# A graph-network kernel on one core: small tables on ScalarE's queue, waits at first use, index transfers ahead of their tiles

## The chip, the core and the metric

The kernel runs on one core of a Trainium2 chip as one program. Its time is the device time of that core in microseconds: 4792.28 us, the median of 3 runs (4786.27 to 4793.47).

The names used here: PE is TensorE, DVE is VectorE, ACT is ScalarE, POOL is GpSimd, SP is SyncE, which only issues transfers. Each has its own instruction stream and its own queue of transfers (its "queue" below); the transfers of all queues are carried out by the core's 16 DMA engines. Between streams there are only semaphores: `.then_inc(sem, n)` raises one when an instruction is done, `wait_ge(sem, v)` holds the stream until it has reached v. All instructions behind a wait in the same stream wait too.

## The reference, cut to what matters

50,000 nodes and 25,000 edges (source, destination; sorted by destination), 128 features, all in fp32. Four layers, each of them added to x, each on h = relu(layernorm(x)):

```python
def gine(h):                        # layer 0
    agg = segment_sum(relu(h[src] + edge_attr), dst)
    y = relu((h + agg) @ W1.T + b1) @ W2.T + b2
    return batchnorm_over_nodes(y) * gamma + beta
def gatv2_conv(h):                  # twice in layer 1, edges plus a self loop per node, 4 heads
    e = einsum(leaky_relu((h @ Wl)[s] + (h @ Wr)[d]), att)
    alpha = softmax of e over the edges of each destination
    return segment_sum(alpha * (h @ Wl)[s], d).mean(heads) + bias
h1 = relu(layer_norm(gatv2_conv(h), g1, be1) + h)       # layer 1
x = x + layer_norm(gatv2_conv(h1), g2, be2) + h1
def gat(h):                         # layer 2, 4 heads of 64, no self loops
    out = relu(softmax-weighted segment_sum of (h @ W_n)[src])
    return relu(out @ mlp_W1 + mlp_b1) @ mlp_W2 + mlp_b2
x = x + 0.5 * segment_sum(h[src], dst) / max(degree, 1)   # layer 3
```

## The kernel before, in words

Nodes are padded to 98 tiles of 512 rows (256 KB each), edges to 49 tiles of 512. The program is a row of phases, each with SBUF, PSUM and semaphores of its own. A phase is one `nc.Block()`, which ends in a barrier on all engines; then `Phase.__exit__` (L53) clears the semaphores on POOL behind a second one (L58). So no instruction of a phase runs before the last one of the phase ahead is done on every engine. POOL's first instruction in a phase is the memset of the identity (`make_identity`, L122), which marks a phase's start in the profile.

In order, with their starts in the profiled execution: gine_edges 0; gine_mlp 563.6; gine_finish 877.5; conv_nodes for the layer-1 convolution 0 at 1159.2 and for the other, called final, at 1447.8; for convolution 0 conv_logits 1722.9, edge_softmax 2251.0, conv_aggregate 2290.7; for convolution 1 the same three at 2604.8, 3133.8 and 3173.5; gat_logits 3545.2; edge_softmax 3875.0; gat_aggregate 3919.2; mean_edges 4282.9.

Inside a phase each engine's stream is written as steps with lags: `sweep(N, [(lag, step), ...])` (L244) runs, for t = 0, 1, ..., step(t - lag) of each pair in the order of the list, where that tile exists. A negative lag runs a step ahead of its tile. SP issues a phase's loads several tiles ahead (rings of 7 node tiles, `tile_in[r]`; of 3 edge tiles in conv_aggregate and gat_aggregate) and its stores.

What a phase needs once, its tables, is loaded at its head. `broadcast_rows` (L98) is one transfer that reads a row of 128 features again for each of 128 partitions, 64 KB in 512-byte pieces. The tables of each phase, all on SP's queue and, but for gine_mlp (after tile 0), ahead of the tile loads:

- gine_mlp (L449): two weights, four columns of 128 (`weights_in`); DVE, PE and ACT wait for all six before anything else.
- gine_finish (L612): the row of the next layer's beta, broadcast four times (`beta_in`), which POOL adds to each tile. POOL's stream: identity, wait for beta, `iota` of row numbers, then for each tile one addition (L641) and one scatter of row numbers into the table POS by an indirect DMA (`scatter_last`, L115).
- conv_nodes (L1410): Wl (256 KB), gamma broadcast, then for convolution 0 beta broadcast four times, the bias row four times; for the final one the bias rows, mlp_row broadcast, the MLP's w2 and b1. DVE sums Wl and the bias into the mean weights `wmean` (L1503 to L1514), PE's first `turn` (transpose) waits for these, `project` (L1489) follows. In the final phase PE also makes a row from relu(b1) and w2 (L1473) ahead of its first tile, and DVE adds it to mlp_row (L1522). In the other POOL looks up POS by a gather (L111) behind each tile's addition.
- conv_logits (L786): Wl, Wr, the eight pieces of the masks KEEP and KEEPN (`Masks.load`, L720), `att`. DVE: wait for the weights, Wl + Wr, centring of Wl by head and its mean (L945 to L958), then two mask scans (L733), then the tiles; PE's first tile waits for the masks' turns (L743).
- conv_aggregate (L1167): gamma, four rows, the bias as a column (`weights_in`, 96 in all). PE, POOL and DVE wait for them at once; PE averages the bias (L1243), DVE centres it (L1325), then `weigh` (alpha by source features) and `project` (L1250) begin. In convolution 0 POOL also looks up POS twice per edge tile.
- gat_logits (L1616): W_n, a_src, a_dst, then the masks. gat_aggregate (L1777): w1, w2, b1; PE and ACT wait for these at once.

## Time and profile before

| | us |
|---|---|
| median of 3 runs | 4792.28 (4786.27 to 4793.47) |
| profiled execution | 4799.01 |
| its span | 4797.0 |
| PE busy in it | 3393.7 (71%) |
| DVE busy | 3285.1 (68%) |
| POOL busy | 2889.3 (60%) |
| ACT busy | 2668.4 (56%) |
| DMA | 1019.82 MB, mean 213 GB/s |

The rows come from one profiled execution. A row of a timeline has the start in us from the span's start, the duration, the engine ("SPq" is the issue of a transfer by SP, not the transfer), the line of the kernel, the operation and its operands (out<-in), how many instructions the row joins, and in brackets how long the engine had been idle before and whose end released it; "PEq" and "POOLq" are the engine's own sequencer at a barrier or a drain. A row of windows has, for a stretch, the busy time of each engine, the granted TensorE clock (1.00 is full), the DMA engines' busy share and their rate.

### The profile page before, as it was taken

The page shows a single profiled execution, that of the slowest core. Times are in us where ns is not written, and L with a number is a line of the kernel's source. Part 1 is how long each engine was busy: PE and PEld are TensorE (multiplying, and loading weights), DVE is VectorE, ACT ScalarE, POOL GpSimd, SP SyncE. Part 2 cuts the span into 40 slices and gives each one's busy share as a digit, 9 for nine tenths or more (in the row PEclk, how much of TensorE's full clock was granted, in tenths as well). Part 3 has the DMA queues.
Part 4 walks back from the last instruction along what each step waited for, and adds up shares of the span by engine and source line. Part 5 has one row for each costly group of instructions (what it writes and reads, how often), then busy time and mean ns, then how long its engine had stood idle before and what let it go on. Part 6 is the DMA issues. An engine that isn't in the chain of part 4 may idle for free. (4 is left out here: it accounts for less than half of the span.)

```text
span 4797.0 us, 66181 instructions
## 1 busy us (share of the span) xinstructions
PE 3393.7 (71%) x14380; PEld 1894.6 (39%) x14380; DVE 3285.1 (68%) x10437; ACT 2668.4 (56%) x7608; POOL 2889.3 (60%) x2835
## 2 busy tenths in 40 slices
PE   1544188544998979997797999948855649974332
PEld 1534133222665633432564344325532215543331
DVE  1322199775996768887786888869978868874332
ACT  1422299796776757775575777726657735530000
POOL 4777687687984457773687555315567600027776
PEclk9656599655999989998898999979978869985555
DMA  8433288796668966664896444459979956753331
GB/s 290 124 97 92 102 282 278 290 406 252 201 190 269 307 194 209 212 212 143 273 323 217 154 158 157 135 195 338 337 239 342 336 164 216 229 185 105 98 99 53
DMA packets 685509, 1019.82 MB, mean 213 GB/s; under 512 B 109779, under 2 KB 293748, under 8 KB 683248
## 3 DMA queue, kind: packets, MB, share of 16 engines
q1 hardware_dynamic: 617296, 877.29, 55.0%
q0 software_dynamic: 65856, 113.13, 9.0%
q10 hardware_dynamic: 2016, 25.69, 1.3%
q8 instruction: 112, 1.84, 0.2%
q14 instruction: 229, 1.88, 0.1%
HBM read 640.44 MB, written 381.14 MB: 213 GB/s over the span
## 5 line engine op out<-in xcount | busy, mean ns | idle before, releaser
L984 DVE TENSOR_TENSOR conv_logits_leaky<-conv_logits_z,conv_logits_sloped 128x512 f32<-128x512 f32 x784 | 516.9, 687 | 117.8 <-ACT conv_logits_sloped L918 102.0
L918 ACT ACTIVATE conv_logits_sloped<-conv_logits_z 128x512 f32<-128x512 f32 x784 | 459.1, 596 | 175.9 <-PE conv_logits_z L880 123.5
L1250 PE MATMUL conv_aggregate_part<-conv_aggregate_weighed,conv_wlc 128*128 128x512 f32 x784 | 360.0, 602 | 39.8 <-DVE conv_aggregate_weighed L1332 39.8
L880 PE MATMUL conv_logits_z<-conv_logits_hdT,conv_logits_wsum 128*128 128x512 f32 x784 | 368.0, 613 | 4.7 <-DVE conv_logits_leaky L984 2.7
L887 PE MATMUL conv_logits_z<-conv_diffT,conv_logits_wl 128*128 128x512 f32 x784 | 352.9, 593 | 0.0
L1570 ACT ACTIVATE conv_nodes_squares<-conv_nodes_o_ps 128x128 f32<-128x128 f32 x784 | 206.5, 278 | 165.7 <-PE conv_nodes_o_ps L1492 165.7
L1332 DVE TENSOR_TENSOR conv_aggregate_weighed<-conv_aggregate_alpha,conv_diffT 128x512 f32<-128x512 f32 x392 | 259.8, 722 | 9.5 <-DMA conv_aggregate_alpha<-ALPHA 9.5
L117 POOL DMA_INDIRECT AGG<-gine_edges_rows,idx x196 | 194.0, 990 | 103.1 <-issue 101.9
L1492 PEld LDWEIGHTS conv_nodes_o_ps<-conv_nodes_wmean,conv_nodes_hT 128*128 128x128 f32 x1568 | 191.3, 192 | 160.3 <-DVE conv_nodes_hT L1528 81.4
L1959 PE MATMUL mean_edges_turned<-mean_edges_ident,mean_edges_hs 128*128 128x128 f32 x196 | 54.6, 434 | 277.7 <-DMA mean_edges_hs<-H,idx 277.7
L111 POOL DMA_INDIRECT gat_logits_hs<-H,idx x196 | 214.4, 1094 | 59.8 <-issue 56.8
L2001 DVE SCALAR_TENSOR_TENSOR mean_edges_rows<-mean_edges_back,mean_edges_half,mean_edges_base 128x128 f32<-128x128 f32 x196 | 55.3, 344 | 276.1 <-DMA out<-mean_edges_rows,idx 273.8
L880 PEld LDWEIGHTS conv_logits_z<-conv_logits_hdT,conv_logits_wsum 128*128 128x128 f32 x784 | 142.9, 192 | 230.1 <-issue 216.6
L1492 PE MATMUL conv_nodes_o_ps<-conv_nodes_wmean,conv_nodes_hT 128*128 128x128 f32 x1568 | 228.9, 289 | 4.3
L117 POOL DMA_INDIRECT out<-mean_edges_rows,idx x196 | 194.7, 993 | 59.7 <-issue 59.0
L111 POOL DMA_INDIRECT gine_edges_hs<-x,idx x196 | 188.6, 962 | 65.3 <-issue 59.4
L1542 DVE SCALAR_TENSOR_TENSOR conv_nodes_scaled<-conv_nodes_o_ps,conv_nodes_rstd,conv_nodes_gamma 128x128 f32<-128x128 f32 x784 | 220.9, 345 | 7.0
L111 POOL DMA_INDIRECT conv_logits_hdx<-HX,idx x196 | 188.3, 961 | 59.9 <-issue 59.9
L111 POOL DMA_INDIRECT conv_logits_hs<-HX,idx x196 | 188.0, 959 | 59.7 <-issue 59.7
L111 POOL DMA_INDIRECT mean_edges_hs<-H,idx x196 | 187.9, 959 | 59.8 <-issue 59.8
L1489 PE MATMUL conv_nodes_o_ps<-conv_nodes_bias,conv_nodes_ones 1*128 1x512 f32 x392 | 221.8, 645 | 0.0
L661 PE MATMUL gine_finish_rows<-gine_finish_ident,gine_finish_bT 128*128 128x128 f32 x392 | 109.1, 434 | 156.9 <-ACT gine_finish_bT L695 155.5
(294 smaller groups left out, 10205.0 us busy)
## 6 DMA issues: line engine op xcount, KB each, us to landing
conv_aggregate_alpha<-ALPHA SPq DMA_DIRECT2D x392, 256.0 KB, 5.3
HX<-gine_finish_hx SPq DMA_DIRECT2D x98, 512.0 KB, 11.7
AGG<-gine_edges_zero ACTq DMA_DIRECT2D x14, 1792.0 KB, 34.2
gine_mlp_x<-x SPq DMA_DIRECT2D x98, 256.0 KB
gine_mlp_agg<-AGG SPq DMA_DIRECT2D x98, 256.0 KB
YT<-gine_mlp_yT SPq DMA_DIRECT2D x98, 256.0 KB, 4.2
gine_finish_x<-x SPq DMA_DIRECT2D x98, 256.0 KB, 7.1
gine_finish_yT<-YT SPq DMA_DIRECT2D x98, 256.0 KB, 11.5
```

Of the source, the lines that this page charges most:

```text
L111: return pool.indirect_dma_start(out=out, out_offset=None, in_=table, in_offset=bass.IndirectOffsetOnAxis(ap=index, axis=0))
L117: return pool.indirect_dma_start(out=table, out_offset=bass.IndirectOffsetOnAxis(ap=index, axis=0), in_=rows, in_offset=None, bounds_check ...
L880: pe.matmul(z[h][:, :], wsum[:, h * D:(h + 1) * D], hdT[j % 3][:, :], start=True, stop=True).then_inc(z_done[0], 1)
L887: pe.matmul(z[h][:, :], wl[:, h * D:(h + 1) * D], g.diffT[:, cols(j)], start=False, stop=True, skip_group_check=True).then_inc(z_done[1], 1)
L918: act.activation(sloped[(H * (2 * j + c) + h) % S][:, :], z[h][:, :], ACT.Copy, scale=SLOPE).then_inc(sloped_made[c], 1)
L984: dve.tensor_tensor(leaky[H * c + h][:, :], z[h][:, :], sloped[(H * (2 * j + c) + h) % S][:, :], ALU.max).then_inc(leaky_made[c], 1)
L1250: last = pe.matmul(part[n % 2][:, :], g.wlc[:, h * D:(h + 1) * D], weighed[n % 2][:, h, :], start=(h == 0), stop=(h == H - 1))
L1332: dve.tensor_tensor(weighed[n % 2][:, h, :], alpha[n % 3][:, h, :], g.diffT[:, n * TILE:(n + 1) * TILE], ALU.mult).then_inc(weighed_made, 1)
L1489: pe.matmul(flat(o), ones[:, :], bias[:, :], start=True, stop=False, skip_group_check=True)
L1492: last = pe.matmul(o[:, a, :], hT[k % 2][:, a * P:(a + 1) * P], wmean[:, :], start=False, stop=True, skip_group_check=True)
L1542: last = dve.scalar_tensor_tensor(out=scaled[r][:, a, :], in0=o_ps[n % 4][:, a, :], scalar=rstd[r][:, a:a + 1], in1=gamma[:, :], op0=ALU.m ...
L1570: last = act.activation(squares[r][:, a, :], o_ps[n % 4][:, a, :], ACT.Square, accum_out=power[r][:, a:a + 1])
```

## The change

Three kinds of edit. **Queue:** the tables listed above are issued by ACT at the head of its stream, in place of SP; in gat_logits and conv_logits that is the masks, the weights staying on SP. **Waits:** each engine waits for them in the step that first reads them. In conv_nodes the tables are split: Wl and the bias rows count on `core_in` and come first, the rest on `weights_in`; PE's row of the final phase moves into a bank of its own and behind the first tiles. In conv_logits the centring of Wl moves behind diff(0). **Look-ahead:** POOL's scatters in gine_finish run 8 tiles ahead of the additions, its gathers in conv_nodes 7 ahead, in conv_aggregate 4 ahead.

```diff
# gine_mlp
-                    if k == 0 and isinstance(i, int) and i == 0:
-                        for dst, src in ((w1, g.w1T), (w2, g.w2T), (b1, g.b1), (b2, g.b2), (gamma, g.gamma), (beta, g.beta)):
-                            sp.dma_start(dst[:, :], src).then_inc(weights_in, 16)
...
                 def copy_y(k, i):
                     r, n = k % RING, i * NB + k
+                    if k == 0 and isinstance(i, int) and i == 0:
+                        dve.wait_ge(weights_in, 6 * 16)
...
                 def first(k, i):
                     n = i * NB + k
+                    if k == 0 and isinstance(i, int) and i == 0:
+                        pe.wait_ge(weights_in, 6 * 16)
...
+                for dst, src in ((w1, g.w1T), (w2, g.w2T), (b1, g.b1), (b2, g.b2), (gamma, g.gamma), (beta, g.beta)):
+                    act.dma_start(dst[:, :], src).then_inc(weights_in, 16)
                 act.wait_ge(eps_set, 1)
-                act.wait_ge(weights_in, 6 * 16)
...
# gine_finish
-                pool.wait_ge(beta_in, 16 * SUB)
-
                 def add_beta(k, i):
                     r, n = k % RING, i * NB + k
                     wait_alone(pool, x1_made, n + 1, own)
+                    if n == 0:
+                        wait_alone(pool, beta_in, 16 * SUB, own)
                     past(pool, out[r], 16 * turns(k, i))
                     pool.tensor_tensor(hx[r][:, :, 1, :], x1[r][:, :, :], beta[:, :, :], ALU.add).then_inc(shifted_made, 1)
 
-                pool.iota(edge_row[:, :, :, :], pattern=[[TILE, g.NTE], [1, 2], [0, 16]], base=g.NP + 2, channel_multiplier=SUB).then_inc(edge_made, 1)
-                for n in range(g.NTN):
-                    add_beta(n % NB, n // NB)
-                    if n == 0:
-                        wait_alone(pool, edge_made, 1, own)
+                def place(n):
                     e, s = n // 2, n % 2
                     scatter_last(pool, g.POS[:, :], g.idx[:, e, 10 + s:11 + s], edge_row[:, e, s, :], g.NP - 1).then_inc(g.placed, 16)
+
+                pool.iota(edge_row[:, :, :, :], pattern=[[TILE, g.NTE], [1, 2], [0, 16]], base=g.NP + 2, channel_multiplier=SUB).then_inc(edge_made, 1)
+                wait_alone(pool, edge_made, 1, own)
+                sweep(g.NTN, [(-8, place), (0, lambda n: add_beta(n % NB, n // NB))])
                 pool.wait_ge(g.placed, 32 * g.NTN)
 
...
+                for a in range(SUB):
+                    broadcast_rows(act, beta[:, a, :], g.conv_norms[1][2], beta_in)
...
# conv_logits, DVE
                 dve.tensor_tensor(wsum[:, :], wl[:, :], wsum[:, :], ALU.add).then_inc(weights_made, 1)
...
                 g.masks.make(dve, masks_in, mask_steps, lead_made, lead_turned, mask_row)
...
+                def centre(j):
+                    if j > 0:
+                        return
...
...
-                sweep(N, [(1, leak(0)), (0, node_moments)] + ([(0, spread_dst)] if spread else []) + [(0, diff), (1, leak(1))] +
+                sweep(N, [(1, leak(0)), (0, node_moments)] + ([(0, spread_dst)] if spread else []) + [(0, diff), (0, centre), (1, leak(1))] +
...
# conv_aggregate
                 def make_base(n):
                     past(pool, res_made, n - 3)
+                    if n == 0:
+                        wait_alone(pool, weights_in, 16 * (2 + SUB), own)
                     wait_alone(pool, hd_in[n % 3], 16 * (n // 3 + 1), own)
...
-                sweep(N, [(0, await_weighed), (4, add_base), (0, make_base), (5, add_row) if final else (0, look_up)])
+                sweep(N, [(0, await_weighed), (4, add_base), (0, make_base), (5, add_row) if final else (-4, look_up)])
...
+                def average(n):
+                    if n == 0:
+                        pe.wait_ge(weights_in, 16 * (2 + SUB))
+                        pe.matmul(hd_ps[0][:, 0:1], avg[:, :], bias[:, :], start=True, stop=True).then_inc(mean_done, 1)
...
+                    if n == 0:
+                        pe.wait_ge(centred_made, 1)
...
+                sweep(N, [(2, combine), (1, turn_dst), (0, average), (0, project)])
...
+                broadcast_rows(act, gamma[:, :], gamma_in, weights_in)
+                for a in range(SUB):
+                    broadcast_rows(act, row[:, a * D:(a + 1) * D], g.mb2 if final else beta_in, weights_in)
+                with nc.allow_non_contiguous_dma("128 biases"):
+                    act.dma_start(bias[:, :], bias_in.rearrange("o d -> d o")).then_inc(weights_in, 16)
...
+                sweep(N, [(3, scale), (0, weigh), (0, centre), (1, scan)] + ([(5, last_stats), (6, last_scales)] if final else []))
...
# conv_nodes
+                    if n == 0 and not final:
+                        wait_alone(pool, weights_in, 16 * n_weights, own)
...
+                def look_up(k, i):
+                    e, s = divmod(i * NB + k, 2)
+                    gather(pool, pos[:, e, s, :], g.POS[:, :], g.idx[:, e, 2 + s:3 + s]).then_inc(g.looked, 16)
+
+                sweep(g.NTN, [(0, at(make_base))] if final else [(-7, at(look_up)), (0, at(make_base))])
...
+                    if n == 0:
+                        pe.wait_ge(bias_step, 3)
+                        pe.wait_ge(wmean_step, 4)
...
+                def make_row(k, i):
+                    if final and i * NB + k == 0:
+                        pe.wait_ge(relu_made, 2)
+                        for j in range(2):
+                            last = pe.matmul(row_ps[:, :], relu_b1[:, j, :], w2[:, j, :], start=(j == 0), stop=(j == 1))
+                        last.then_inc(c_done, 1)
...
+                sweep(g.NTN, [(lag, at(step)) for lag, step in [(0, turn), (1, project), (2, make_row)]])
...
-                dve.wait_ge(weights_in, 16 * n_weights)
+                dve.wait_ge(core_in, 16 * (1 + SUB))
...
+                    if n == 0:
+                        dve.wait_ge(weights_in, 16 * n_weights)
...
+                steps = ([] if final else [(0, copy_turned)]) + [(2, invert), (2, scale), (2, relu_bias), (3, finish), (5, add_row)]
...
+                act.dma_start(wl[:, :], g.conv_weights[layer][0]).then_inc(core_in, 16)
+                for a in range(SUB):
+                    act.dma_start(bias[:, a * D:(a + 1) * D], bias_in).then_inc(core_in, 16)
+                broadcast_rows(act, gamma[:, :], gamma_in, weights_in)
+                if not final:
+                    for a in range(SUB):
+                        broadcast_rows(act, beta[:, a * D:(a + 1) * D], beta_in, weights_in)
+
+                if final:
+                    broadcast_rows(act, g.mlp_row[:, :], g.mb2, weights_in)
+                    act.dma_start(w2[:, :, :], g.mw2.rearrange("(j p) n -> p j n", p=P)).then_inc(weights_in, 16)
+                    with nc.allow_non_contiguous_dma("256 biases"):
+                        act.dma_start(b1[:, :], g.mb1.rearrange("o (j p) -> p (o j)", p=P)).then_inc(weights_in, 16)
...
# gat_aggregate
                 def first(n):
+                    if n == 0:
+                        pe.wait_ge(weights_in, 48)
...
+                act.dma_start(w1[:, :, :], g.mw1.rearrange("(j p) n -> p j n", p=P)).then_inc(weights_in, 16)
+                act.dma_start(w2[:, :, :], g.mw2.rearrange("(j p) n -> p j n", p=P)).then_inc(weights_in, 16)
+                with nc.allow_non_contiguous_dma("256 biases"):
+                    act.dma_start(b1[:, :], g.mb1.rearrange("o (j p) -> p (o j)", p=P)).then_inc(weights_in, 16)
                 act.wait_ge(weights_in, 48)
```

The tables' own code, `relu_bias` (the memset and relu(b1)) and `add_row` (the addition to mlp_row) keep their instructions; the masks' loop in `Masks.load` is unchanged but for the engine that issues it.

## Rows read from the trace of the kernel before

**Rows 1.** Four windows (busy us, count; clock; DMA share; GB/s)

```profile
core 0: us, PE busy (x) PEld busy (x) DVE busy (x) ACT busy (x) POOL busy (x), PEclk, DMA share, GB/s
1000.00:1040.00 40.00, 16.70 (x60) 10.74 (x60) 30.66 (x181) 38.18 (x91) 33.70 (x31) 0.50 1.04 405
1300.00:1340.00 40.00, 39.24 (x210) 24.48 (x209) 39.47 (x106) 29.00 (x148) 37.42 (x30) 1.00 0.64 198
2000.00:2040.00 40.00, 40.00 (x164) 16.07 (x160) 32.61 (x92) 31.40 (x65) 30.42 (x32) 1.00 0.65 210
2450.00:2490.00 40.00, 39.88 (x198) 26.08 (x197) 36.26 (x71) 29.27 (x106) 35.15 (x30) 1.00 1.02 328
```

**Rows 2.** Timeline, gine_mlp head: start, us, engine line op [idle before <-releaser]

```profile
564.44 0.42 SPq L449 DMA_DIRECT2D gine_mlp_w<-w1T  x1
...
569.31 0.87 DVE L142 BATCH_NORM_STATS2 gine_mlp_norm_stats<-gine_mlp_x 128x6 f32<-128x128 f32 x4 [5.59 <-DMA gine_mlp_beta<-beta]
```

**Rows 3.** Timeline, gine_finish's head

```profile
877.49 1.76 SPq L100 DMA_DIRECT2D gine_finish_beta<-cbe  x4
...
887.26 1.87 POOL L643 IOTA gine_finish_edge_row<- 128x1568 int32 x1 [9.11 <-DMA gine_finish_beta<-cbe]
...
888.61 0.81 ACT L695 ACTIVATE gine_finish_bT<-gine_finish_yT,bn_shift,bn_scale 128x512 f32<-128x512 f32 x1 [12.69 <-DMA gine_finish_yT<-YT]
```

**Rows 4.** Three windows of gine_finish, columns as before

```profile
883.00:885.00 2.00, 0.00 (x0) 0.00 (x0) 0.00 (x0) 0.00 (x0) 0.00 (x0) 0.50 0.25 37
887.00:889.00 2.00, 0.00 (x0) 0.00 (x0) 0.00 (x0) 0.39 (x1) 1.74 (x1) 0.50 1.06 408
1150.00:1158.00 8.00, 0.00 (x0) 0.00 (x0) 0.00 (x0) 0.00 (x0) 0.00 (x0) 0.50 0.00 0
```

**Rows 5.** Timeline, gine_finish's tail and the next identity

```profile
1144.41 2.78 SPq L626 DMA_DIRECT2D HX<-gine_finish_hx  x2
...
1146.96 0.99 POOL L117 DMA_INDIRECT POS<-gine_finish_edge_row,idx  x1 [0.17 <-issue]
...
1159.21 0.20 POOL L122 MEMSET conv_nodes_ident<- 128x128 f32 x1 [11.26 <-POOLq L58]
```

**Rows 6.** Timeline, heads of the two conv_nodes phases

```profile
1170.06 1.02 DVE L1503 TENSOR_REDUCE conv_nodes_heads<-conv_nodes_wl 128x128 f32<-128x512 f32 x1 [10.60 <-DMA conv_nodes_bias<-cb]
...
1454.02 1.02 DVE L1503 TENSOR_REDUCE conv_nodes_heads<-conv_nodes_wl 128x128 f32<-128x512 f32 x1 [5.92 <-DMA conv_nodes_b<-mb]
...
1459.64 1.97 PE L1482 MATMUL conv_nodes_turned<-conv_nodes_ident,conv_nodes_h 128*128 128x128 f32 x8 [0.38 <-DVE mlp_row L1522]
```

**Rows 7.** Timeline of POOL inside conv_nodes of layer 0

```profile
1184.75 0.96 POOL L111 DMA_INDIRECT conv_nodes_pos<-POS,idx  x1 [0.17 <-issue]
...
1430.52 1.29 POOL L1453 TENSOR_TENSOR conv_nodes_base<-conv_nodes_h,conv_nodes_beta 128x512 f32<-128x512 f32 x1
...
1431.97 1.24 POOL L111 DMA_INDIRECT conv_nodes_pos<-POS,idx  x1 [0.17 <-issue]
```

**Rows 8.** Timeline, head of conv_logits of layer 0

```profile
1727.67 0.58 SPq L791 DMA_DIRECT2D conv_logits_att<-att1T  x1
...
1732.19 0.69 DVE L944 TENSOR_TENSOR conv_logits_wsum<-conv_logits_wl,conv_logits_wsum 128x512 f32<-128x512 f32 x1 [9.07 <-DMA conv_logits_att<-att1T]
...
1735.76 1.78 DVE L733 TENSOR_TENSOR_SCAN masks_lead<-masks_keep 128x784 f32<-128x784 f32 x1
```

**Rows 9.** Timeline, head of conv_aggregate of layer 0

```profile
2301.00 0.56 PE L1243 MATMUL conv_aggregate_hd_ps<-conv_aggregate_bias,conv_aggregate_avg 128*128 128x1 f32 x2 [21.83 <-DMA conv_aggregate_bias<-cb]
```

**Rows 10.** Timeline, heads of gat_logits and gat_aggregate

```profile
3553.75 1.79 DVE L733 TENSOR_TENSOR_SCAN masks_lead<-masks_keep 128x784 f32<-128x784 f32 x1 [2.69 <-DMA masks_keep<-KEEPN]
...
3926.45 0.69 DVE L1874 TENSOR_TENSOR gat_aggregate_part<-gat_aggregate_y,gat_aggregate_alpha 128x512 f32<-128x512 f32 x1 [7.05 <-DMA gat_aggregate_alpha<-ALPHA]
```

**Rows 11.** Timeline of DVE in gine_edges

```profile
27.08 0.47 DVE L338 CAST gine_edges_rowf<-gine_edges_rowi 128x588 f32<-128x588 int32 x1 [22.45 <-DMA gine_edges_rowi<-next_r]
```

**Rows 12.** The page's DMA issues: KB each, us from issue to landing

```profile
AGG<-gine_edges_zero ACTq DMA_DIRECT2D x14, 1792.0 KB, 34.2
```

120 lines of the change are left out of this document (41 added, 79 removed).

## The prediction

> **What bounds the kernel now.** The page's engine shares come first and settle little: no engine is over 71% busy, because the program is a row of phases with different limits, each closed by a barrier. So the next view is one window in the middle of each long phase [rows 1]. There the limits are plain. gine_finish is held by the DMA engines (share 1.04, 405 GB/s) and almost by ACT (38.18 of 40 us). conv_nodes of layer 0 has PE, DVE and POOL all within 3 us of full. conv_logits of layer 0 is PE alone, at the full clock, with POOL just behind it: 32 instructions, each gather followed by a gap in its own issue. conv_aggregate has PE at 39.88 and DMA at 1.02. The change touches none of this: per tile the same instructions and transfers remain. What it can move is the edges of phases, so the third view is the timeline around each phase's first instructions, where I look for the engine that starts last and what released it. Almost everywhere it is a small table: the bias of conv_nodes, waited for 10.60 us [rows 6], the beta rows of gine_finish, 9.11 us [rows 3], `att` in conv_logits, 9.07 us [rows 8], the bias column in conv_aggregate [rows 9]. The last view is the end of gine_finish [rows 4, 5]. The profiled execution took 4799.0 us, 0.14% over the median of 4792.3; all sums are made against 4799.0 and then carried over.
>
> **The change part by part.** All terms are gains at a phase's head or tail, minus signs mean shorter.
>
> gine_mlp: six table issues of about 0.47 us leave SP ahead of tile 1, 2.8 us, and the first statistics no longer wait for beta, which released them at 569.31 [rows 2]. POOL and ACT follow tile by tile. Gain 2.4, bounds 1.5 and 3.5.
>
> gine_finish, head: the four beta broadcasts are issued at 877.49; until about 885 the DMA engines are a quarter busy at 37 GB/s, while the tile loads stand behind them on one queue, and the rate jumps to 408 GB/s afterwards [rows 4]. ACT starts on the first tile at 888.61 [rows 3]. On another queue the loads use the three quarters that lie idle: 0.75 x 6.5 = 4.9 us in a phase that DMA bounds. Eight look-ahead scatters of 0.99 + 0.17 [rows 5] now stand on POOL before its first addition, 9.3 us behind the IOTA, so POOL is free at about 889.5; its first addition was at 891.6 and its buffers give it a few tiles of room, so this hides. Head 5, bounds 3 and 7.
>
> gine_finish, tail: SP issues its last store until 1147.19, POOL its last scatter until 1147.95; from 1150 to 1158 no engine and no DMA does anything, and the next phase opens at 1159.21 after 11.26 us idle on POOL [rows 4, 5]. So about 9 us pass on POOL alone after its last indirect transfer has landed. I take these 9 us as fixed and coming after whatever POOL does last; what changes is when it does that. Without scatters between the last eight additions it is up to 9.3 us earlier, until it waits for DVE's tiles; with the head's 5 us, POOL's last work ends at 1136 to 1140 and its idle stretch at 1145 to 1149, while the last store lands at about 1145. Tail 7, bounds 4 and 9.
>
> conv_nodes, layer 0: ten tables of about 0.4 us stood before the loads, and DVE began the mean weights at 1170.06 [rows 6], 10.9 us after the phase opened. Now it waits for five of them only, issued first. The second conv_nodes phase, which has two broadcasts in place of five, shows all its tables landed 6.2 us after its start (wait of 5.92, start of DVE at 1454.02 [rows 6]). So the five land 5 to 6 us after the opening, 5 to 6 us saved; and PE turns tile 0 before the mean weights instead of after, 1.9 us. The seven look-ups in front, some 8.5 us on POOL, end by 1168.5, before beta can be there, and its first addition is not needed until finish(0). Gain 8, bounds 5 and 10.
>
> conv_nodes, final: DVE's start moves up by 1.5; the four row matmuls and their addition, about 2 us ahead of PE's first turn at 1459.64 [rows 6], go into the stream, where PE has to pay 0.6 to 1.2 back. The turn before the mean weights brings 1.9 again. Gain 5, bounds 3 and 7.
>
> conv_logits, both layers: `att` is issued at 1727.67 behind eight mask transfers of about 0.45 (0.42 and a gap, as in [rows 2]), 3.6 us, and DVE starts at 1732.19; the mask scan comes at 1735.76 after 3 us of centring [rows 8]. Both go from the path: up to 6.5. It doesn't all arrive: the masks themselves must have landed, and in layer 0 POOL gathers back to back through the phase (8 gathers of 0.95 with 0.3 between are 10.1 us per tile, PE's pace too [rows 1]), so that it can follow by some 5.7 at most. Gain 3.9 in layer 0 (2 to 5.7) and 4.8 in layer 1 (3 to 6). Centring now lies behind diff(0), where DVE would wait for PE's first products anyway; uncovered it would cost its 3 us, once per layer.
>
> conv_aggregate, both layers: `average` now stands before PE's first projection and still waits for the bias, the last of six transfers; it ran at 2301.00 [rows 9]. So the bias still gates; what goes is the wait behind it for alpha, whose issue moves up by 2.7 us and out of the broadcasts' way. The look-ups four tiles ahead take about 9 us of POOL that is idle until the first weighing. Gain 3 each, bounds from 3 lost (the tables slowed by loads beside them) to 5.
>
> gat_logits: the scan waits for the masks themselves at 3553.75 [rows 10]; only the loads behind them move up, and POOL's gathers bind next. Gain 1, bounds 0 and 3.7. gat_aggregate: alpha lands for 3926.45 [rows 10] and is issued 1.5 us earlier. Gain 1.4, bounds 0 and 3. gine_edges, the softmaxes and mean_edges don't change.
>
> Sum: 2.4 + 12 + 8 + 5 + 3.9 + 4.8 + 3 + 3 + 1 + 1.4 = 44.5 us. 4799.0 - 44.5 = 4754.5 for an execution like the profiled one; from the median 4792.3 - 44.5 = 4748. Best ends together give 65 (4727), worst ends 16 (4776).
>
> **The rivals.**
>
> *Issue time only.* The tables land when they did, because they need the same DMA engines, and only SP's issue slots are saved: 2.8 + 1.8 + 4 + 3.5 + 3.6 + 2.7 + 3.7 + 2.7 + 0 + 1.5 = 26.3, plus the tail's 7: 33, hence 4759. For it: in conv_aggregate the bias gates as before. Against it: the quarter-busy DMA in rows 4. The Trainium skill, "Trainium Kernel Development and Optimization", Key Constraints, has this rule: DMAs of SP, ACT and POOL share 16 engines, and several issuers save issue time only. By that rule the sum would be this rival's; the trace agrees that engines are shared, but shows them idle behind a slow transfer.
>
> *POOL's pace in conv_nodes.* The tile took 1.45 + 1.24 = 2.69 us on a POOL without waits [rows 7], while an early gather took 0.96. Shifted by seven tiles, gathers may fall beside other DVE work. At 0.96 POOL would need 2.41 and PE, at 39.24 of 40 us [rows 1], would hold the tile at 2.6: 0.09 less on 98 tiles, 9 us; I price the bad side alike. To the good 4739, to the bad 4757. Against it: the mix per tile stays the same.
>
> *The scatter tail isn't POOL's.* If the 9 us follow the last store instead, the tail gives 0 to 1: 4754. This lies in the forecast's own range.
>
> *Nothing arrives.* Every table is still waited for early, and the loads, once ahead, only wait in full buffers: only the waits moved in conv_nodes and conv_logits count, about 10 us, 4782. For it: rings of seven tiles fill fast. Against it: gine_finish and conv_aggregate are at a DMA share of 1.0, where an idle microsecond is lost.
>
> *Slower: tables starved beside tiles.* One mechanism: while both queues have work, an engine alternates between them, and each small packet of a table waits for a large one of a tile. In gine_edges three row broadcasts issued from 1.3 us on were not complete until 27.08 [rows 11], beside ACT's 1792-KB zero stores [rows 12]: some 24 packets per engine, about 1 us each beside packets of 14 KB. The tiles' packets are of 2 KB, a seventh, so 0.15 us on each of 32 to 40: 5 us late. The gates are beta in gine_finish and conv_nodes, and the bias in the two conv_aggregates: four places. It turns the sign from 44.5 / 4 = 11 us of lateness in each; with the full 1 us for some 15 of the packets, 15 us, the sum is 44.5 - 60, 15 us slower: 4808. The Trainium skill, "DMA: Bandwidth & Descriptors", Queues, rings and completion order, says that an engine drains a packet of about 9 to 17 descriptors before it goes to the other ring. By it a table's turn could wait for a dozen tile rows, which is how lateness of that size would come; no row here shows it for these tiles.
>
> **How the numbers follow.** Chances: forecast with its tail variant 0.64 (own range 4733 to 4762), issue only 0.15, POOL's pace 0.08, nothing arrives 0.08, starved tables 0.05. The range 4728 to 4774 leaves out the far half of the last two and a little beyond the best ends. A change within 0.2% (9.6 us) can't be told from none. Faster: everything of the first three and half of "nothing arrives", 0.90; same 0.05; slower 0.05.
>
> **What would show it.** Of each phase, the distance from its identity to the same instruction: the mean weights in conv_nodes 5 to 6 us after it instead of 10.9; ACT's first tile in gine_finish 4 to 5 us after it, not 11.1; DMA share near 1 in the first 6 us there; the mask scan in conv_logits 6 to 8 us after it, not 12.9. POOL's idle stretch before conv_nodes should still be 9 us or more but start before 1141. `average` should still start 10 us into conv_aggregate. Windows in mid-phase should not change. The forecast is wrong if the phases' heads shorten and their ends don't (a pace that changed, or a bound reached later), or if `average` comes at 15 us or more.

## The result, and the profile after

The changed kernel takes 4783.6 us (median of 12 runs, 4777.5 to 4793.3) where the kernel before took 4792.8 (12 runs beside it): a ratio of 0.9979, interval 0.9970 to 0.9988. By the medians that is 9.2 us faster, a fifth of the 44.5 that the prediction summed, and the time is above the range that it gave. The profiled execution's span is 4784.4 us, against 4797.0.

The next rows are the identity's memset, one form for each name with its count, the min/median/max of one in ns, and the first and last start in us. From these and from the same rows of before come the phases' lengths below.

```profile
L122 POOL MEMSET gine_finish_ident<- x1: 204/204/204, 876.4 to 876.4; 128x128 f32 x1
...
L122 POOL MEMSET conv_nodes_ident<- x2: 204/204/205, 1148.3 to 1432.5; 128x128 f32 x2
...
L122 POOL MEMSET conv_logits_ident<- x2: 205/206/206, 1712.8 to 2591.8; 128x128 f32 x2
...
L122 POOL MEMSET conv_aggregate_ident<- x2: 204/204/204, 2281.5 to 3160.2; 128x128 f32 x2
...
L122 POOL MEMSET gat_logits_ident<- x1: 204/204/204, 3531.4 to 3531.4; 128x128 f32 x1
```

| phase, us | before | after | difference | predicted | mean of more profiles |
|---|---|---|---|---|---|
| gine_mlp | 313.9 | 312.1 | -1.8 | -2.4 | -1.6 |
| gine_finish | 281.7 | 271.9 | -9.8 | -12 | -9.8 |
| conv_nodes, layer 0 | 288.6 | 284.2 | -4.4 | -8 | -6.2 |
| conv_nodes, final | 275.1 | 280.3 | +5.2 | -5 | -0.5 |
| conv_logits, layer 0 | 528.1 | 528.9 | +0.8 | -3.9 | +0.2 |
| conv_aggregate, layer 0 | 314.1 | 310.3 | -3.8 | -3 | -6.4 |
| conv_logits, layer 1 | 529.0 | 528.7 | -0.3 | -4.8 | -0.3 |
| conv_aggregate, layer 1 | 371.7 | 371.2 | -0.5 | -3 | +0.9 |
| gat_logits | 329.8 | 333.0 | +3.2 | -1 | +2.6 |
| gat_aggregate | 363.7 | 361.6 | -2.1 | -1.4 | -2.0 |
| untouched phases together | | | +0.9 | 0 | |

gine_finish alone gives 9.8 of this pair's 12.6 us. The other nine phases, forecast at 32.5, give 3.7 together.

The last column uses every profile in which the phase's code was that of one kernel or the other, but for those of the last chip named below: two of before, four to eight of after. The second profile of before was one of its longest executions (4812), so these means flatter the change (they add up to 23 us); they are good for order, not for tenths. That chip has one more profile of each code of conv_nodes in layer 0, and there the order is the other way round: 285.1 us before (`finish_ahead_only`), 297.3 after (`bias_first`).

gine_finish did what was forecast. ACT's first tile and the end of the phase in the profile after:

```profile
883.10 0.81 ACT L694 ACTIVATE gine_finish_bT<-gine_finish_yT,bn_shift,bn_scale 128x512 f32<-128x512 f32 x1 [8.32 <-DMA gine_finish_yT<-YT]
...
1136.94 2.54 POOL L638 TENSOR_TENSOR gine_finish_hx<-gine_finish_x,gine_finish_beta 128x512 f32<-128x512 f32 x2 [0.59 <-DMA HX<-gine_finish_hx]
...
1137.18 5.14 SPq L623 DMA_DIRECT2D HX<-gine_finish_hx  x4
...
1148.29 0.20 POOL L122 MEMSET conv_nodes_ident<- 128x128 f32 x1 [8.81 <-POOLq L58]
```

ACT begins 6.7 us into the phase (11.1 before [rows 3]). POOL's last additions end at 1139.48, and the next phase opens 8.81 us later: this idle stretch does follow POOL's own last instruction, as the prediction took it from [rows 5], not the last store, whose issue ends at 1142.3. In all eleven profiles where an addition is POOL's last instruction it is 8.8 us; in the three where a scatter is, 11.3 to 11.8. In the head the DMA engines do more from the start, though not all that they could; the columns are those of [rows 1]:

```profile
881.00:883.00 2.00, 0.00 (x0) 0.00 (x0) 0.00 (x0) 0.00 (x0) 1.70 (x2) 0.50 0.55 169
887.00:889.00 2.00, 1.12 (x4) 0.72 (x4) 0.03 (x1) 0.81 (x2) 1.39 (x3) 0.50 1.04 393
```

Conv_nodes of layer 0 shows the head's gain as forecast too, with one difference:

```profile
1152.73 1.02 DVE L1503 TENSOR_REDUCE conv_nodes_heads<-conv_nodes_wl 128x128 f32<-128x512 f32 x1 [4.18 <-DMA conv_nodes_bias<-cb]
...
1162.35 1.13 DVE L1548 SCALAR_TENSOR_TENSOR conv_nodes_scaled<-conv_nodes_o_ps,conv_nodes_rstd,conv_nodes_gamma 128x128 f32<-128x128 f32 x4 [0.63 <-DMA conv_nodes_beta<-cbe]
...
1162.51 1.26 POOL L1451 TENSOR_TENSOR conv_nodes_base<-conv_nodes_h,conv_nodes_beta 128x512 f32<-128x512 f32 x1 [3.17 <-DMA conv_nodes_beta<-cbe]
```

The mean weights start 4.4 us after the phase opened (10.9 before [rows 6]). But gamma and beta, last of ten on ACT's queue, come at 14 us: the first scaling waits 0.6 us and POOL 3.2 us for them. Its first addition now starts 14.2 us into the phase; before it was 11.9.

### The profile page after: what moved, and what is told of

Same layout as the page of the kernel before. It is cut to its first block and busy times, and to the rows that moved or that the text cites. A ratio compares the mean times of both kernels' runs of the same rounds, so it can differ in the third digit from the quotient of the medians.

```text
span 4784.4 us, 66192 instructions
## 1 busy us (share of the span) xinstructions
PE 3407.1 (71%) x14380; PEld 1906.6 (40%) x14380; DVE 3271.7 (68%) x10437; ACT 2658.1 (56%) x7608; POOL 2869.4 (60%) x2835
## 5 line engine op out<-in xcount | busy, mean ns | idle before, releaser
L1342 DVE TENSOR_TENSOR conv_aggregate_weighed<-conv_aggregate_alpha,conv_diffT 128x512 f32<-128x512 f32 x392 | 257.0, 715 | 23.5 <-DMA conv_aggregate_alpha<-ALPHA 23.5
L1485 PE MATMUL conv_nodes_o_ps<-conv_nodes_wmean,conv_nodes_hT 128*128 128x128 f32 x1568 | 239.0, 298 | 0.0
L111 POOL DMA_INDIRECT conv_logits_hs<-H,idx x196 | 189.7, 968 | 53.9 <-issue 48.2
## 6 DMA issues: line engine op xcount, KB each, us to landing
HX<-gine_finish_hx SPq DMA_DIRECT2D x98, 512.0 KB, 11.8
AGG<-gine_edges_zero ACTq DMA_DIRECT2D x14, 1792.0 KB, 34.3
```

What stands on the lines that cost most here:

```text
L111: return pool.indirect_dma_start(out=out, out_offset=None, in_=table, in_offset=bass.IndirectOffsetOnAxis(ap=index, axis=0))
L1342: dve.tensor_tensor(weighed[n % 2][:, h, :], alpha[n % 3][:, h, :], g.diffT[:, n * TILE:(n + 1) * TILE], ALU.mult).then_inc(weighed_made, 1)
L1485: last = pe.matmul(o[:, a, :], hT[k % 2][:, a * P:(a + 1) * P], wmean[:, :], start=False, stop=True, skip_group_check=True)
```

## The experiments

They are told in the order run. Ratios are to the kernel before on the same chip. The first four ran on one chip (kernel before: 4791 us), the next four on a second (4801), the last four on a third (5156), where POOL's stream of gathers in conv_logits of layer 0 has gaps that it has nowhere else: 44 over 0.45 us, 124 us together, in `finish_ahead_only`, none in the profile of before. The changed kernel without an edit was not timed on the last two. So ratios rank variants of one chip; across chips single phases have to do it, and on the third only those that the gathers do not stretch.

**A second profile of the changed kernel** (`after_again`, no edit).

> The changed kernel once more, for a second profile. Its first profile had TensorE at 1.2 GHz until 42 us into conv_nodes of layer 0 and until 34 us into the final one, with PE busy from about 7 us on in both; before the change the clock rose at 20 and 18 us, 6 to 7 us after PE had begun. Theory C (the way PE enters these phases keeps the clock low): the long low stretches are there again, within some 10 us of the same place. Rival L (chance): at least one of the two clocks rises within 15 us of PE's start, and that phase is 5 to 13 us shorter than in the first profile (284.2 and 280.3).

4784.3 us, ratio 0.9986 (0.9976 to 0.9995). The clock rose at 18 and 21 us, and the final phase took 274.6 us: chance, as rival L says. But layer 0 took 287.8 us, longer than in the first profile with the clock low for 42 us, which neither theory had.

**Order of PE's first instructions in conv_nodes** (`nodes_order`).

```diff
                 pe.wait_ge(ident_made, 1)
+                pe.wait_ge(bias_step, 3)
+                pe.wait_ge(wmean_step, 4)
```

> The changed kernel, but in both conv_nodes phases PE waits for the mean weights and the bias before its first transposes, as it did before the change; then the first two tiles' eight transposes run back to back. Theory C: the clock rises 6 to 8 us after PE's start, conv_nodes of layer 0 takes 270 to 276 us instead of 284, the final one 268 to 272 instead of 280: some 18 us off the total, about 4765. Rival L (chance) and rival D (the tables' and loads' traffic, or the lag of the row matmuls, keeps it low): the clock stays low as long as in the changed kernel and the phases keep 284 and 280 within 2 us, or one of them changes at random.

4782.9 us, 0.9984 (0.9975 to 0.9993): no gain. The clock rose at 18 and 21 us, where it rose for the unedited code in its second profile. The phases took 294.1 and 274.7. Theory C falls. The 294.1 led to the stall. These are POOL, DVE and PE 256 us into conv_nodes of layer 0:

```profile
1404.79 6.14 POOL L1451 TENSOR_TENSOR conv_nodes_base<-conv_nodes_h,conv_nodes_beta 128x512 f32<-128x512 f32 x5
...
1405.70 5.79 DVE L1555 TENSOR_TENSOR conv_nodes_scaled<-conv_nodes_scaled,conv_nodes_base 128x512 f32<-128x512 f32 x1
...
1412.14 1.22 PE L1484 MATMUL conv_nodes_o_ps<-conv_nodes_wmean,conv_nodes_hT 128*128 128x128 f32 x4 [4.90 <-DVE conv_nodes_hT L1531]
```

Five additions of POOL run on end, since no look-up is left between them, and one DVE addition that takes 0.68 us elsewhere takes 5.79 beside them, ending just after the fifth. PE stands 4.9 us for the copy behind it, and its clock falls to 1.2 GHz for most of what is left. Of the first five profiles of kernels with this look-ahead only the first had nothing of it; the others had DVE additions of 4.57, 5.79, 5.79 and 5.80 us there. Neither profile of before had one. In the first profile of the changed kernel POOL's additions at this place each wait 1.30 us for DVE: POOL is ahead, and no run forms. In the others POOL works without a wait and is behind, and when the look-ups end it catches up in one run.

**Warming PE** (`nodes_preheat`).

```diff
                 pe.wait_ge(ident_made, 1)
+                for j in range(32):
+                    pe.matmul(o_ps[3][:, j % SUB, :], ident[:, :], ident[:, :], start=True, stop=True)
```

> The changed kernel, with 32 more 128x128 matmuls of the identity by itself (into a bank that the fourth tile overwrites) at the head of PE's stream in both conv_nodes phases; nothing else uses them. They take about 8 us at 1.2 GHz, from 0.7 us on, and so end 1 to 2 us after tile 0 could have begun. Theory C: the clock is full by about 8 to 10 us into each phase, the low stretches are gone, and conv_nodes takes 268 to 274 us in layer 0 and 264 to 270 us in the final one. Rival D: the clock doesn't follow what PE does in front; the phases get 1 to 2 us longer than 284 and 280.

4785.4 us, 0.9991 (0.9980 to 1.0001). The clock is full 6 to 7 us into both phases, and the final one takes 272.4 us, 2.2 less than with an ordinary rise. Theory C missed the lengths, 268 to 274 and 264 to 270: layer 0 took 289.0, stall included. So the clock does follow PE, and it isn't what holds layer 0. The median has nothing of the warm-up: 4785.4 beside 4784.3 of the unedited kernel.

**Three heads** (`three_heads`): masks of gat_logits on SP ahead of the tiles; the bias column first and alone in conv_aggregate; scatters of gine_finish behind their tiles.

```diff
-                g.masks.load(act, g, masks_in)          # gat_logits
...
+                g.masks.load(sp, g, masks_in)           # behind the weights, ahead of the tile loads
...
-                        pe.wait_ge(weights_in, 16 * (2 + SUB))
+                        pe.wait_ge(column_in, 16)       # conv_aggregate; DVE's centre too
...
-                sweep(g.NTN, [(-8, place), (0, lambda n: add_beta(n % NB, n // NB))])
+                sweep(g.NTN, [(0, lambda n: add_beta(n % NB, n // NB)), (0, place)])
```

> The changed kernel with three edits in phases that don't touch each other. gat_logits: the masks back on SP's queue ahead of the tile loads. Theory S (tables land later when tile loads stand beside them on another queue): the first mask scan comes 8.5 to 9.5 us into the phase instead of 13.5, and the phase takes 329 to 330 us instead of 333.0. Rival: the scan moves, the phase stays at 333, because DMA bounds it. conv_aggregate, both: the bias column first on ACT's queue with a semaphore of its own, PE's average and DVE's centring wait for it alone, gamma for the first scaling. Theory S: average runs by 7 us into the phase (11.7 and 13.3 now), and the first projection follows the first weighing; layer 0 gains 1 to 3 us, layer 1 3 to 6. Rival: DMA at a share of 1.0 gives it back, under 1 us each. gine_finish: each scatter behind its tile's addition again, the broadcasts left on ACT's queue. Prediction's step: the tail's 7 us come back (279 instead of 271.9). Rival: the head gave it all, 272 to 273.

4793.6 us, 1.0006 (0.9997 to 1.0015). gine_finish 279.2: taken away from the changed kernel the look-ahead costs 7.5 of its 9.8 us; the broadcasts' queue by itself is worth 2.3. gat_logits 327.0, its scan at 9.7 us: theory S holds, and the phase follows. conv_aggregate 316.2 in layer 0 (worse, neither theory) and 367.8 in layer 1 (3.4 better). The profiled execution was the shortest of its runs (4782.7), so its phases can't be added up to the median.

**The kernel before again** (`before_again`).

> The kernel before once more, for a second profile, to see how far a phase's length differs between executions of the same code. If one look is good to 1 us, all phases agree with the first profile within 1 us and its span is 4797 again; if the phases with coupled engines (conv_nodes, conv_aggregate) have more than one pace, they differ by 2 to 10 us while gine_mlp, gine_finish and conv_logits agree.

One run, 4812.1 us. gine_mlp, gine_finish, both conv_logits and gat_logits agree within 1.0 us. conv_nodes took 297.2 and 280.7 (8.6 and 5.6 more), conv_aggregate 318.2 and 368.8 (4.1 more, 2.9 less), gat_aggregate 360.8 (2.9 less). So the long low clock belongs to neither kernel. One window each, 20 to 40 us into conv_nodes of layer 0, before, before again, after, after again:

```profile
1179.20:1199.20 20.00, 20.00 (x106) 12.43 (x105) 17.96 (x46) 13.65 (x77) 18.53 (x17) 0.98 0.43 124
```
```profile
1178.10:1198.10 20.00, 20.00 (x57) 12.33 (x58) 10.44 (x29) 6.87 (x41) 14.51 (x13) 0.50 0.23 57
```
```profile
1168.30:1188.30 20.00, 20.00 (x61) 12.66 (x60) 15.05 (x29) 7.32 (x39) 18.60 (x17) 0.50 0.27 75
```
```profile
1169.30:1189.30 20.00, 20.00 (x110) 12.67 (x108) 19.15 (x47) 14.48 (x78) 18.60 (x16) 1.00 0.51 157
```

PE is busy without a break in all four. At a granted 0.50 it does 57 to 61 matmuls in 20 us, at 1.00 106 to 110. A tile takes 4.86 us at 1.2 GHz and 2.6 to 2.7 at 2.4 GHz, so each microsecond at the low clock costs 0.45.

**Look-ups behind their tiles again** (`nodes_no_ahead`).

```diff
-                sweep(g.NTN, [(0, at(make_base))] if final else [(-7, at(look_up)), (0, at(make_base))])
+                sweep(g.NTN, [(0, at(make_base))] if final else [(0, at(make_base)), (0, at(look_up))])
```

> The changed kernel, but in conv_nodes of layer 0 each look-up stands behind its tile's addition again, as before the change; the tables stay on ACT's queue. In three profiles with look-ahead POOL made five additions back to back 256 us into the phase (6.1 us) and one DVE addition of 0.68 us took 5.8 beside them; PE then stood 4.9 us and its clock fell. Theory P (POOL's unbroken additions shut DVE out of the memory port that both use; the gathers used to break them up): no DVE addition over 1.3 us in the phase, the clock stays full to the end of PE's work, and DVE's last addition comes 5 to 8 us earlier; but POOL's last gather and drain are late again, so the phase takes 280 to 284 us instead of 284 to 294. Rival T (the look-ahead is worth the tail): the phase takes as long or longer, 286 to 290, as POOL's drain ends it.

4786.9 us, 0.9968 (0.9955 to 0.9981). No DVE addition over 1.51 us: the stall is gone, so it takes the look-ahead to make it. But the phase took 288.3: POOL's last addition starts at 274.3 us, its last gather at 275.7, and gather, copy and drain set the end. Theory P holds on the stall and rival T on the phase.

**A shorter leash** (`nodes_leash`).

```diff
-                    past(pool, sum_made, n + 1 - RING)
+                    past(pool, sum_made, n + 1 - 4)
```

> The changed kernel with the look-ahead kept, but POOL's addition for tile n waits until DVE has finished tile n-4 instead of n-7, in both conv_nodes phases. So POOL can't have several additions in a row at the end. Theory P: the stall of about 5 us at 256 us is gone or under 2 us, and conv_nodes of layer 0 takes 279 to 284 us. Rival Q (the stall comes from the look-ahead's end itself or from the DMA queue, whatever the additions' order): it stays, 284 to 294.

4778.3 us, 0.9955 (0.9941 to 0.9969). In that profile, at the place of the stall:

```profile
1402.35 2.50 POOL L1451 TENSOR_TENSOR conv_nodes_base<-conv_nodes_h,conv_nodes_beta 128x512 f32<-128x512 f32 x2
...
1403.27 2.14 DVE L1556 TENSOR_TENSOR conv_nodes_scaled<-conv_nodes_scaled,conv_nodes_base 128x512 f32<-128x512 f32 x1
```

Two additions on end at most, the DVE addition 2.14 us instead of 5.8, and the phase takes 282.4. Theory P holds in its mechanism: in every profile the DVE addition is as long as POOL's run beside it (2.14, 3.36, 4.57, 5.79 us for two, three, four, five). How much of it is the leash's doing is less sure, for `masks_sp` below, without one, had a run of two as well (2.13 us), and `bias_first` of three.

**Masks between weights and tiles on SP** (`masks_sp`; in gat_logits as above, in conv_logits the same line behind `att`).

> The changed kernel with the mask pieces on SP's queue again, but behind the weights (and att) and ahead of the tile loads, in both conv_logits and in gat_logits. Theory S (tables land late beside tile loads on another queue): in conv_logits of layer 1 the mask scan starts 9 to 10 us into the phase instead of 12.6 and the phase takes 525 to 527 us instead of 528.7; gat_logits takes 327 to 330 us instead of 331 to 334; conv_logits of layer 0 keeps 528 to 529 in any case, since POOL's gathers set its pace from its first microsecond. Rival: the scans move and no phase gets shorter by more than 1 us.

4783.0 us, 0.9963 (0.9951 to 0.9975), against the leash's 0.9955 and 0.9968 without look-ahead on this chip. The first mask scans of conv_logits in layer 1 and of gat_logits, after the change and in this kernel (PE's row is the averaging in conv_aggregate of layer 1):

```profile
2604.10 1.79 DVE L732 TENSOR_TENSOR_SCAN masks_lead<-masks_keep 128x784 f32<-128x784 f32 x1 [4.97 <-DMA masks_keep<-KEEPN]
...
3173.49 0.56 PE L1243 MATMUL conv_aggregate_hd_ps<-conv_aggregate_bias,conv_aggregate_avg 128*128 128x1 f32 x2 [24.78 <-DMA conv_aggregate_bias<-cb]
...
3544.88 1.79 DVE L732 TENSOR_TENSOR_SCAN masks_lead<-masks_keep 128x784 f32<-128x784 f32 x1 [3.59 <-DMA masks_keep<-KEEPN]
```

```profile
2597.65 1.80 DVE L732 TENSOR_TENSOR_SCAN masks_lead<-masks_keep 128x784 f32<-128x784 f32 x1 [2.94 <-DMA masks_keep<-KEEPN]
...
3533.79 1.79 DVE L732 TENSOR_TENSOR_SCAN masks_lead<-masks_keep 128x784 f32<-128x784 f32 x1 [2.46 <-DMA masks_keep<-KEEPN]
```

From the identities at 2591.8 and 3531.4, and 2588.9 and 3524.2: the scans start 12.3 and 13.5 us in with the masks on ACT's queue, 8.7 and 9.6 with them on SP's. Before the change they started at 12.2 and 8.6, but in layer 1 behind 3 us of centring: DVE's wait for `att`, issued behind the masks, had ended at 8.6. The phases take 524.5 and 328.6 us: theory S holds. conv_logits of layer 0 took 530.6, a little over the 528 to 529 expected.

**One edit on the kernel before** (`finish_ahead_only`): the scatters of gine_finish 8 tiles ahead, nothing else.

> The kernel before with one edit: the scatters of gine_finish run 8 tiles ahead of the additions; the beta broadcasts stay on SP's queue and everything else is as before. Adding the terms measured so far (271.7 with both edits, 279.2 with the queue alone, 281.4 with neither): 273 to 275 us for the phase if the tail's 7 us are the look-ahead's own, and the total 0.1 to 0.2% under the kernel before. Rival: the two edits need each other (the eight scatters in front can't start before beta has landed), 279 or more.

Ratio 0.9979 (0.9968 to 0.9990), 11 us, phase 274.5 us. So this one edit gives here what the whole change gave on the first chip. `bias_first`, which is nearly the whole change, gives 22 us here, and its gine_finish takes 267.7: beside the look-ahead the broadcasts' queue is worth 6.8 us, not 2.3, for with beta on SP's queue the eight scatters in front start only behind it and POOL's first addition comes at 23.5 us instead of 14.6. The rival was right in part: the two edits help each other. conv_logits of layer 0 took 671.5 us instead of 528, with the same instructions; its middle:

```profile
2102.00:2142.00 40.00, 34.25 (x135) 14.20 (x132) 25.40 (x79) 24.74 (x53) 23.67 (x26) 0.96 0.50 160
```

**The bias first** (`bias_first`, that edit of `three_heads` alone).

> The changed kernel with the bias column first on ACT's queue in both conv_aggregate phases and PE's average and DVE's centring waiting for it alone. One look together with other edits gave 316.2 us in layer 0 (310 with the bias last, in five looks 307.7 to 310.4) and 367.8 in layer 1 (369.9 to 373.0). Theory M (the start decides which of two paces layer 0's coupled POOL and DVE fall into, 5.8 or 6.0 us per tile, and the earlier start falls into the slow one): 314 to 318 again in layer 0, 366 to 369 in layer 1. Rival L (chance): layer 0 at 306 to 309.

Ratio 0.9958 (0.9945 to 0.9972). Layer 0 308.0, layer 1 367.9. Theory M falls: layer 0 starts as early as in `three_heads` and is 8 us shorter, so the 316.2 is not the early start's doing; layer 1 repeats 367.8. The averaging and the first projection there:

```profile
3428.71 0.56 PE L1244 MATMUL conv_aggregate_hd_ps<-conv_aggregate_bias,conv_aggregate_avg 128*128 128x1 f32 x2 [15.63 <-DMA conv_aggregate_bias<-cb]
...
3432.60 6.68 PE L1250 MATMUL conv_aggregate_part<-conv_aggregate_weighed,conv_wlc 128*128 128x512 f32 x8 [3.32 <-DVE conv_aggregate_weighed L1343]
```

They stand 4.1 and 8.0 us after the phase's opening at 3424.6; after the change the averaging ran at 13.3.

**Leash and masks together, without and with the warm-up** (`combined`, `combined_warm`).

> The changed kernel with the two edits that helped: POOL's additions in conv_nodes at most four tiles ahead of DVE, and the masks on SP's queue between the weights and the tile loads. If the phases add: conv_nodes of layer 0 at 282 to 284, conv_logits of layer 1 at 524.5 to 526, gat_logits at 328 to 330, in all 6 to 10 us under the changed kernel, 0.9955 to 0.994 of the kernel before. Rival: the clock's late rises, which come by chance, blur it to nothing (0.998).

> The same as combined, with the 32 extra matmuls at the head of PE's stream in both conv_nodes phases, which took TensorE to the full clock 6 us into each. Theory L (the late rise of the clock comes by chance in either kernel and costs 0.45 us for each us that PE works at 1.2 GHz): conv_nodes at 281 to 283 and 271 to 273 in the profile, and over the rounds a narrower spread and a median 2 to 6 us under combined. Rival: the profile looks better and the median doesn't move.

Ratios 0.9950 (0.9936 to 0.9963) and 0.9939 (0.9926 to 0.9953); medians 5128.7 and 5121.3 beside 5156.1. Both beat the kernel before; the changed kernel was not timed on this chip, and `bias_first` is at 5134.2. Little is left of the masks' gain here: conv_logits of layer 1 takes 541.0 and 542.7 us, and 541.7 with the masks on ACT's queue; gat_logits 360.2 and 361.0 against 362.2. The spread didn't narrow with the warm-up (9 us, 8 without). Its 7 us in the median are more than expected, and what makes them isn't shown: the unedited kernel gained nothing by it. The two profiled executions differ by 14.6 us, 8.8 of them in conv_nodes of layer 0, 275.1 us instead of 283.9, and that is not the clock alone. The gathers of this phase, min/median/max in ns, in the changed kernel's second profile, its first, and `combined_warm`:

```profile
L111 POOL DMA_INDIRECT conv_nodes_pos<-POS,idx x98: 943/1231/1243, 1150.4 to 1403.5; - x98
```
```profile
L111 POOL DMA_INDIRECT conv_nodes_pos<-POS,idx x98: 944/957/1232, 1149.4 to 1393.1; - x98
```
```profile
L111 POOL DMA_INDIRECT conv_nodes_pos<-POS,idx x98: 943/960/1247, 1248.0 to 1491.3; - x98
```

There are two paces: 2.69 us per tile with gathers of 1.23 us, 2.58 with gathers of 0.96. Nine of the eleven profiles of changed kernels ran at the first pace after some 14 tiles, the first profile and this one at the second throughout; all three with the code of before ended in the first. On 98 tiles that is 10.8 us, which is how the changed kernel's first profile could have PE 24 us longer at the low clock (11 us) than its second and still be the shorter.

## Why the prediction was wrong, step by step

The sums are right; what failed was the step from a head that starts earlier to a phase that ends earlier. That step was made phase by phase without asking what the bounding engine had already been doing during the head, or whether the tables would land when they used to. Nearly all that came is gine_finish. The rival "nothing arrives" has almost the measured number, 4782, but by luck: it counts on conv_nodes and conv_logits alone and leaves gine_finish out.

*gine_mlp, gine_finish, gat_aggregate*: right, -1.8, -9.8, -2.1 for 2.4, 12 and 1.4. The tail term of 7 measured 7.5, by the step as put: POOL's 9 us follow its own last instruction. The head's 5 was 2.3: with beta on the other queue the loads ran at 169 GB/s and not at 400, so that ACT's first tile came 4.4 us earlier and its last 2.1. POOL got beta no sooner; its first addition stands at 14.6 us, 14.1 before. The variant in which the tail follows the last store is out.

*conv_logits, layer 0* (3.9 forecast, none found). The step that failed is "it can follow by some 5.7": I took PE's window of 40.0 of 40 us [rows 1] as PE the bound and POOL as its follower with slack. The rows say otherwise. POOL's 392 gathers run from the phase's first microsecond to 497.0 us after the change and to 495.6 before, with no gap over 0.45 us; PE only keeps up with them. The last gather and PE's last product after, and then before:

```profile
2209.78 0.95 POOL L111 DMA_INDIRECT conv_logits_hs<-HX,idx  x1 [0.31 <-issue]
...
2233.07 1.07 PE L895 MATMUL conv_logits_dots<-conv_logits_leaky,conv_logits_att 128*32 128x512 f32 x8 [0.42 <-DVE conv_logits_leaky L987]
```

```profile
2218.47 0.95 POOL L111 DMA_INDIRECT conv_logits_hs<-HX,idx  x1 [0.31 <-issue]
...
2242.35 1.06 PE L897 MATMUL conv_logits_dots<-conv_logits_leaky,conv_logits_att 128*32 128x512 f32 x8 [0.42 <-DVE conv_logits_leaky L984]
```

From the last gather to the last product it is 23.3 us after and 23.9 before. The scan moved by 3.4 us and nothing followed, in `masks_sp` neither, where it stands at 9.6 us too. On the third chip, where the gathers' stream has its gaps, the phase stretched by 143 us with PE at 34.3 of 40. The prediction had these gathers in a row; it took their equal pace for room to follow.

*conv_logits, layer 1, gat_logits, conv_aggregate of layer 1* (gains of 4.8, 1 and 3 forecast; 0.3 gained, 3.2 lost, 0.5 gained). What failed is that the forecast let the moved tables land no later than they had: the masks came 12.3 and 13.5 us into their phases (by 8.6 in both before), the bias 11.7 and 13.3 in the two conv_aggregates (10.3 and 10.4), because the tile loads that used to stand behind them now ran beside them. In conv_aggregate of layer 1 the wait behind the bias did go, as forecast, and the lateness took just that back: the first projection runs at 13.7 us in both kernels. The direction was in the rival of starved tables, which I priced at 5 us for each and gave 0.05. Late tables were real in these four phases, by 1.4 to 4.9 us (how the engines share the packets isn't shown); putting the masks back (`masks_sp`, `three_heads`) gives 4.2 us in conv_logits of layer 1 and 3.8 to 5.4 in gat_logits, the bias first (`bias_first`) 3.2 in conv_aggregate of layer 1. The Trainium skill's rule that several issuers save issue time only ("Trainium Kernel Development and Optimization", Key Constraints) is thereby too kind to such a change: by these rows a table moved beside the bulk loads can land later than it did ahead of them.

*conv_nodes, layer 0* (8 forecast; 4.4 in the pair, 6.2 in the means of the table). The head gave its 8 us to PE and DVE: the first scaling runs at 14.0 instead of 21.6. Of these the low clock took a random part in both kernels, and look-ahead made the stall, 5 us and the clock behind it. The prediction let the seven look-ups hide ahead of the first addition; it didn't ask what they had been doing where they stood, between the additions. Whether the phase gained at all isn't shown: with the code of before it took 288.6, 297.2 and 285.1 us, with the changed code unedited 284.2, 287.8, 286.9, 288.0 and 297.3. With the leash it took 282.4, and 283.9 in `combined`, shorter than each of before.

*conv_nodes, final* (5 forecast, 5.2 lost in the pair). The loss was the clock: 27 us of PE work at 1.2 GHz against 8.3, 19 x 0.45 = 8.5 us. It came with the code of before too (18.0 us, 280.7; 22.9 us, 281.9). With 0.45 us taken off for each of these microseconds the phase is 271.4, 272.6 and 271.6 in three profiles with the code of before, 267.7 to 269.1 in six with the changed code: about 3.3 of the 5 arrived. The prediction has no term for the clock; it let the one profile's low stretch stand.

*conv_aggregate, layer 0* (3 forecast, 3.8): the number is right, not proven to be for the reason given. The first projection came 1.8 us earlier. Between tiles 10 and 40 a tile takes 5.65 to 5.69 us in eleven profiles, 5.74 to 5.90 in three: both of before and `three_heads`. At the short tile the code of before takes 311.6 us (`finish_ahead_only`), the changed one 307.7 to 310.4 in nine profiles, so 1 to 4 us are the change's and the rest is the pace.

Of the rivals, "POOL's pace" was the nearest to what conv_nodes does; it was priced at 9 us, and the two paces are 10.8 apart. The forecast's own test, that the phases' heads shorten and their ends don't, is what came in most of them. The range failed since the worst ends, which summed to 16, allowed a loss only in conv_aggregate: the late masks, the low clock and the stall had no term.

## What to carry to other kernels

Before you credit a head, look for an engine that works without a wait from the phase's first microsecond to near its last (here POOL's gathers): no table that others wait for is worth anything then, however idle the rest look. When you move an instruction out of a stream, ask what it separated there as well as what it delayed. And take two profiles of the kernel before: a term smaller than what two profiles of the same phase differ by can't be forecast from one.

## What the runs showed of the hardware

POOL additions on end shut a DVE addition out for as long as they last: 0.68 us alone, 0.93 beside one, 2.14 beside two, 3.36 beside three, 4.57 beside four, 5.79 beside five; in the rows of `nodes_order` and `nodes_leash` it ends 0.6 us after POOL's run. The Trainium skill ("SBUF — State Buffer", SBUF: two separate sides) has DVE and GpSimd share a pair of ports by an exclusive lock, held for a whole instruction, a DVE instruction with two SBUF inputs beside a GpSimd one that reads SBUF among the cases. The trace agrees on the lock, but one instruction is 1.27 us and DVE waited for up to five: POOL seems to get it again when its next instruction is ready.

TensorE's clock stayed at 1.2 GHz for 7 us of work in one profile of conv_nodes in layer 0 of the kernel before and for 36 us, without a break in PE's work, in the other. 32 matmuls without gaps ahead of the work had it at 2.4 GHz 4 to 7 us into the phase in all four phases that had them; in two of them, both in `combined_warm`, it fell once more for 3 to 7 us and came back.

A phase in which POOL issued indirect transfers ends with a drain of POOL's own of 8.05 us or more, in gine_finish after the change 9.2 us, though its last scatter ended 17 us before the drain began; in the final conv_nodes, which has none, the drain takes 1.36 us (profiles of both kernels).

What holds the clock low in some executions, and what picks one of two paces in conv_nodes and conv_aggregate, stays open. That the pace hangs on how POOL's and DVE's additions fall beside each other is argued from the gathers' two lengths, not shown.
